# Three token tiles under the first expert's weights, and a PSUM bank shared with the adapter, in a two-layer conditional kernel

## The reference

```python
# layer 0: 8 gated experts and one shared expert, all applied to all tokens, F = 512
g = einsum('bsd,edf->ebsf', h, Wg);  u = einsum('bsd,edf->ebsf', h, Wu)
expert_outs = einsum('ebsf,efd->ebsd', silu(g) * u, Wd)
expert_output = einsum('be,ebsd->bsd', gating_probs, expert_outs)
shared = einsum('bsf,fd->bsd', silu(h @ Sg) * (h @ Su), Sd)
x = x + (1 - sg) * expert_output + sg * shared
# layer 1: an adapter per sequence, its weights chosen by language_ids; then a layer norm with gamma, beta
h1 = relu(x @ W1[lang] + b1[lang])
z = x + h1 @ W2[lang] + b2[lang]
x = x + layernorm(z) * gamma[lang] + beta[lang]
```

## Time and profile before

| | |
|---|---|
| median of 3 runs | 305.44 us (305.38 to 305.45) |
| the profiled execution, its own time | 304.87 us |
| its span, first to last instruction | 303.1 us |
| TensorE matmul busy | 295.1 us, 97% of the span |
| VectorE busy | 264.4 us, 87% |
| ScalarE busy | 226.6 us, 75% |
| GpSimd busy | 15.9 us, 5% |
| mean granted TensorE clock | 0.996 of full speed |

### The profile page before, as it was taken

One profiled execution on the slowest core, in us unless ns is written; L12 is line 12 of the kernel. 1 busy time (PEld: TensorE's weight loads), 2 busy tenths in 40 slices (PEclk: granted clock), 3 DMA queues, 4 the chain that ended last, 5 costly groups with the idle time before them and its releaser, 6 DMA issues.

```text
span 303.1 us, 4961 instructions
## 1 busy us (share of the span) xinstructions
PE 295.1 (97%) x1532; PEld 147.5 (49%) x1532; DVE 264.4 (87%) x590; ACT 226.6 (75%) x505; POOL 15.9 (5%) x24
## 2 busy tenths in 40 slices
PE   8999999999999999999999999999999999999983
PEld 3344444444444444444444444444444444688862
DVE  5999999998989898987779998699987899888894
ACT  5897878788878787877677776777777676688761
POOL 0200101200000000000010100101001010000000
PEclk9999999999999999999999999999999999999998
DMA  7990000014400000000000010000000000100000
GB/s 248 414 404 11 0 0 2 9 38 121 121 11 0 2 0 0 0 2 2 0 8 13 0 37 0 1 14 7 35 0 2 10 9 0 37 1 2 3 17 17
DMA packets 9133, 12.12 MB, mean 40 GB/s; under 512 B 3843, under 2 KB 6804, under 8 KB 9108
## 3 DMA queue, kind: packets, MB, share of 16 engines
q1 hardware_dynamic: 8962, 11.75, 11.3%
q10 hardware_dynamic: 146, 0.07, 0.1%
HBM read 10.76 MB, written 1.05 MB: 39 GB/s over the span
## 4 chain that ended last, share of the span: by engine, by line
PE 89%; issue 3%; DVE 1%; POOLq 0%; POOL 0%; DVEq 0%; ACT 0%
PE moe_ps L328 10%; PE moe_ps L330 10%; PE gate_ps L287 10%; PE moe_ps L327 10%; PE up_ps L309 10%; PE up_ps L312 10%; PE gate_ps L293 10%; PE gate_ps L290 10%; PE up_ps L306 10%; PE adapt_ps L353 1%; PE adapt_ps L340 1%; PE x_ps L345 1%; DVE hidden L500 0%; DVE h_lo L506 0%; DVE gx_lo L481 0%
## 5 line engine op out<-in xcount | busy, mean ns | idle before, releaser
L426 ACT ACTIVATE silu<-gate_ps 128x512 f32<-128x512 f32 (+1 forms) x160 | 88.6, 554 | 64.1 <-PE gate_ps L293 63.5
L500 DVE SCALAR_TENSOR_TENSOR hidden<-silu,up_ps 128x512 f32<-128x512 f32 (+1 forms) x160 | 100.7, 630 | 28.7 <-PE up_ps L312 22.6
L506 DVE TENSOR_TENSOR h_lo<-hidden,h_hi 128x512 f16<-128x512 f32 (+1 forms) x160 | 101.5, 635 | 0.1
L431 ACT ACTIVATE h_hi<-hidden 128x512 f16<-128x512 f32 (+1 forms) x160 | 92.8, 580 | 2.5 <-DVE hidden L500 2.2
L330 PE MATMUL moe_ps<-h_lo,w_hi 128*128 128x512 f16 (+1 forms) x160 | 57.3, 358 | 0.9 <-DVE h_lo L506 0.8
L309 PE MATMUL up_ps<-gx_lo,w_hi 128*128 128x512 f16 (+1 forms) x160 | 57.3, 358 | 0.7 <-DVE gx_lo L481 0.7
L287 PE MATMUL gate_ps<-x_hi,w_hi 128*128 128x512 f16 (+1 forms) x160 | 57.7, 360 | 0.0
L293 PE MATMUL gate_ps<-x_hi,w_lo 128*128 128x512 f16 (+1 forms) x160 | 57.5, 360 | 0.0
L290 PE MATMUL gate_ps<-x_lo,w_hi 128*128 128x512 f16 (+1 forms) x160 | 57.5, 360 | 0.0
L306 PE MATMUL up_ps<-gx_hi,w_hi 128*128 128x512 f16 (+1 forms) x160 | 57.3, 358 | 0.1
L327 PE MATMUL moe_ps<-h_hi,w_hi 128*128 128x512 f16 (+1 forms) x160 | 57.3, 358 | 0.0
(11 more groups left out here) (74 smaller groups left out, 146.4 us busy)
## 6 DMA issues: line engine op xcount, KB each, us to landing
w_full<-weights SPq DMA_DIRECT2D x8, 768.0 KB, 10.8
affine_sb<-affine SPq DMA_DIRECT2D x16, 128.0 KB, 2.9
x_full<-xT SPq DMA_DIRECT2D x4, 256.0 KB, 6.4
w_full<-weights SPq DMA_DIRECT2D x3, 256.0 KB, 4.3
out_dram<-result SPq DMA_DIRECT2D x3, 256.0 KB, 2.0
w2b_sb<-w2b SPq DMA_DIRECT2D x16, 16.5 KB
w_sb<-w SPq DMA_DIRECT2D x16, 16.0 KB
b_sb<-b SPq DMA_DIRECT2D x16, 0.1 KB
```

The costliest lines, as they stand in the source:

```text
L426: nc.scalar.activation(pair_slot(silu, n), gate_ps[n % 2][:, 0:STEPS[n][4]], ACT.Silu, scale=1.0 / W_SCALE).then_inc(silu_ready, 1)
L431: nc.scalar.activation(h_slot(h_hi, n), pair_slot(hidden, n), ACT.Copy).then_inc(h_hi_ready, 1)
L500: nc.vector.scalar_tensor_tensor(out=pair_slot(hidden, n), in0=pair_slot(silu, n), scalar=HIDDEN_RESCALE, in1=up_ps[n % 2][:, 0:STEPS[n][4 ...
L506: nc.vector.tensor_tensor(h_slot(h_lo, n), pair_slot(hidden, n), h_slot(h_hi, n), ALU.subtract).then_inc(h_lo_ready, 1)
```

## The change

Expert 0 is applied to tiles 0, 1 and 2 before expert 1 is begun; tile 2 so has its first group as steps 8 to 11, and all groups of tiles 0 and 1 with experts 1 to 8 come one group later. The count of groups, steps and matmuls stays. The weights of expert 1 are converted at steps 6, 8 and 10, not at 4, 5 and 6; those of the later experts keep their place within the turn. Tile 2 must be loaded and split early, so its load moves ahead of the load of expert 1, and `X_AFTER[2]` falls from 9 to 3. Tile 2's sum begins while those of tiles 0 and 1 are still open, so it gets a bank of its own, `moe_ps2`, and the adapter writes into `moe_ps0`, which is free from the end of tile 0 on. The second half of tile 3 uses tile 2's bank. Because `JOBS` is worked out from the steps, the jobs of tiles 0 and 1 start 4 steps later.

```diff
-GROUPS = [(t, e) for e in range(NE) for t in (0, 1)] + [(2, e) for e in range(NE)] + [(3, e) for e in range(NE)]
+FIRST = [(t, 0) for t in (0, 1, 2)]
+GROUPS = (FIRST + [(t, e) for e in range(1, NE) for t in (0, 1)] + [(2, e) for e in range(1, NE)]
+          + [(3, e) for e in range(NE)])
...
-W_AT = {2 * CHUNKS * e + s: (e + 1, third) for e in range(NE - 1)
-        for third, s in enumerate((4, 5, 6) if e == 0 else (2, 4, 6))}
-
-X_AFTER = {1: 2, 2: 9, 3: 12}
+W_AT = {s: (1, third) for third, s in enumerate((6, 8, 10))}
+W_AT |= {CHUNKS * (len(FIRST) + 2 * (e - 1)) + s: (e + 1, third) for e in range(1, NE - 1)
+         for third, s in enumerate((2, 4, 6))}
+
+X_AFTER = {1: 2, 2: 3, 3: 12}
...
-        moe_ps = [bank("moe_ps0"), bank("moe_ps1")]
-        adapt_ps = bank("adapt_ps")
+        moe_ps = [bank("moe_ps0"), bank("moe_ps1"), bank("moe_ps2")]
+        adapt_ps = moe_ps[0]
...
-        last_moe_ps = moe_ps[0]
+        last_moe_ps = moe_ps[2]
...
-            return moe_ps[0] if at > 0 else moe_ps[t % 2]
+            return last_moe_ps if at > 0 else moe_ps[1 if t == TILES - 1 else t]
...
             sp.dma_start(cols(w_full, 2, F), weights[0, :, 2 * F:]).then_inc(w0_loaded[2], 16)
+            sp.dma_start(cols(x_full, 2, N), xT[2]).then_inc(x_loaded[2], 16)
             for e in range(1, NE):
                 sp.dma_start(cols(w_full, e, W_COLS), weights[e]).then_inc(w_loaded[e - 1], 16)
-                if e in (2, 3):
-                    sp.dma_start(cols(x_full, e, N), xT[e]).then_inc(x_loaded[e], 16)
+                if e == 3:
+                    sp.dma_start(cols(x_full, 3, N), xT[3]).then_inc(x_loaded[3], 16)
...
-                if f == 0 and e == 0 and t > 1:
-                    pe.wait_ge(x2T_ready, t - 1)
+                if f == 0 and e == 0 and t == TILES - 1:
+                    pe.wait_ge(x2T_ready, 2)
...
-                nc.vector.scalar_tensor_tensor(out=x2T[:, :], in0=moe_ps[t % 2][:, :], scalar=OUT_RESCALE,
+                nc.vector.scalar_tensor_tensor(out=x2T[:, :], in0=moe_bank(t, 0)[:, :], scalar=OUT_RESCALE,
```

## The result

The changed kernel takes 306.11 us (median of 7 runs, 305.86 to 306.45) against 305.38 us (7 runs, 304.87 to 305.45); the ratio worked out from all runs of both is 1.0029, 95% interval 1.0019 to 1.0039 (the quotient of the two medians alone is 1.0024). Of the twelve runs of experiment 3, two took 522.31 and 1771.03 us, for a reason that no trace here shows; its ratio leaves them out. The profiled execution has a span of 304.1 us, 303.1 before.

What follows compares the result with a forecast made beforehand. TensorE was taken to bound the kernel, with VectorE's lateness before 13.81 us having no slack. The collision's +1.00 us and zero for all else, added to 305.44, gave 306.44 us, range 305.4 to 306.9.

Steps and rivals of the forecast that it cites:

- What bounds the kernel: TensorE 97% busy, gapless from 14.70 to 285.00 us; at step 4 it loses about 0.7 us waiting for VectorE.
- the last critical quarters: Group 1's last gx_lo quarters on VectorE, ending at 13.81 us; step 4's second up matmul waits for them.
- The collision: GpSimd's early split of tile 2, from 10.49 us, holds VectorE's h_lo 0.10 and gx_lo 0.90: +1.00 us.
- The rival of the full lock: Both GpSimd instructions hold VectorE for their whole length near 10.5 us: +1.38, total 306.82 us; chance 0.14.
- Edits costed at nothing: Order, matmul count, loads, banks, jobs and later conversions of expert 1's weights: each claimed to cost or gain 0.
- the relief at steps 4 and 5: Converting expert 1 later lightens VectorE and ScalarE where TensorE never waits: gain 0; rival that it counts, 304.75 us, chance 0.04.
- the nearest of the covers: Tile 2's adapter weights, issued until 213.4 us and wanted at 228.69 + 1.0: covered by 16 us, cost 0.
- The sum: Total +1.00 us on the median of 305.44 us: 306.44 us, 0.33% slower.
- the likeliest case: Whole kernel at 306.44 us, with its own range from 306.1 to 306.8; chance 0.57.
- the tail's clock is safe: Between 294 and 297 us TensorE is busy 1.62 of 3.00 us, clock 1.00; rival of falling clock, 309.2 us, chance 0.04.

Runs made afterwards that it cites:

- experiment 3: Changed kernel with only GpSimd's subtraction for tile 2 held back until group 1's gx_lo is done, its copy left early; 305.46 us, ratio 1.0001.
- experiment 1: Changed kernel with GpSimd's whole split of tile 2 held back until group 1's last gx_lo quarters are done; 305.44 us, ratio 1.0000.
- experiment 2: Kernel before with two edits alone: tile 2's x loaded right behind expert 0, and X_AFTER[2] = 3; 306.52 us, ratio 1.0034.
- experiment 7: Kernel before with X_AFTER[2] = 3 alone, tile 2's x still loaded behind expert 2; 305.95 us, ratio 1.0037.
- experiment 6: Changed kernel with expert 1's weights converted at steps 4, 5 and 6 as before, not at 6, 8 and 10; 306.43 us, ratio 1.0038.

## Why the prediction was right

- *What bounds the kernel.* TensorE without a gap from step 4 on, VectorE without slack before it: experiments 1, 2 and 7 put nearly the same loss of VectorE (1.02, 0.99 and 0.90 us) after, before and just at the last critical quarters, and the total followed the place alone.
- *The collision.* Predicted copy at 10.49, `hidden(2)` at 13.01, pair at 14.21, second up matmul at 14.86; measured 10.49, 12.99, 14.19, 14.85. The loss of 1.00 us, taken from the earlier trace rows, was 0.98. The trace of before held the same four instructions in the same phase; where the phase was another, in experiment 7, the loss was 0.90. The rival of the full lock, +1.38, is refuted: the lock is there, but it lets the leads of experiment 3 through.
- *Edits costed at nothing.* Order, banks, jobs, loads, and the relief at steps 4 and 5: experiments 1 and 6 confirm zero. Tile 2's adapter weights, the nearest of the covers, were issued until 213.70 and wanted at 229.67:

```profile
213.70 0.32 SPq L262 DMA_DIRECT2D b_sb<-b  x1
```

- *The sum.* 306.44 was forecast, 306.11 measured. Most runs of a sample lie near one of two levels: those of before near 304.88 and 305.45, those of after near 305.86 and 306.45, with 305.21, 306.11 and 306.29 in between. Level against level the change costs 0.98 and 1.00 us; the medians of 7 give 0.73. The forecast added 1.00 to a median of three runs that all lay on the upper level, and this choice was not argued. That the measured median still lies within the likeliest case's own range, at its lower edge of 306.1, depends on how the seven runs fell and not on the mechanism.
- *What I had wrong.* That the tail's clock is safe: I argued from the earlier trace rows that the granted clock stays at 1.00 although TensorE is busy only 1.62 of 3.00 us there. Experiment 1's tail shows it falling after just such a stretch. It didn't touch this prediction, because the idle stretches that the change makes, 0.57 and 0.66 us at step 4, left the clock at 1.00. TensorE's busy time from 8.6 to 15.7 was forecast at 5.5 us and came to 5.87. The forecast had added the whole 1.00 to the idle time; but a matmul that stands alone between two waits counts as busy for its 0.38 us and not for the 0.22 to the next start. The rest is that TensorE's short wait at step 3 had gone and its stream reached step 4 0.11 us later (below).

## What to carry to other kernels

A wait count that releases a GpSimd instruction is also a choice of which VectorE instructions it will hold; look at what VectorE does just then and how much slack it has. Held here were those with all inputs in SBUF; `hidden`, with one in PSUM, kept its 0.68 us beside both GpSimd instructions. The cost of a moved collision could be read here off the place in the trace where the same instructions already collide, to a few hundredths, because the phase agreed. And where TensorE waits for one of two results that VectorE makes one after the other, try their order first: one swap was worth 0.5 us of the span here, about 0.2%, the whole regrouping nothing.

## What the runs showed of the hardware that was not expected

**The clock can fall in the tail.** In the last steps TensorE works with gaps. In the profile of before the granted clock was still 1.00 between 297 and 298 us, in that of experiment 1, with the same tail, it was 0.65 (the column before the last two):

```profile
297.00:298.00 1.00, 1.00 (x9) 0.66 (x8) 0.31 (x2) 0.68 (x2) 0.00 (x0) 1.00 0.00 0
```

```profile
297.00:298.00 1.00, 1.00 (x7) 0.83 (x7) 0.17 (x1) 0.69 (x2) 0.00 (x0) 0.65 0.00 0
```

After it the clock was 0.50, that is 1.2 GHz, and the span 0.8 us longer; experiment 6's profile shows the same fall. The idle times of TensorE before it were no longer than 0.48 us each. That the two levels of the timed runs, some 0.57 us apart, are this fall, is not shown, because those runs have no trace, and it can't be all of it. Each run has its mean granted clock on record. Of the 25 runs of the kernel before that stand beside experiment 1, the ten at 304.87 to 304.90 us had 0.996 to 0.998. Eleven of the fifteen slower ones had 0.989 to 0.994, which fits a fall in the tail (0.989 in experiment 1's profile), but four, at 305.21 to 305.45, had 0.998 or 0.999. And in the sample of the changed kernel the four slower runs had the higher clock, 0.997 or 0.998 against 0.995 or 0.996. A late rise at the start, which follows, could be behind these; no trace shows one that costs so much.

**A late rise of the clock costs nothing at first.** Matmuls 0.43 us apart went on until about 6.8 us in the profile of before and until 8.5 in experiment 3. In the changed kernel `hidden(0)` started at 8.82, 0.39 later than before, and yet `hidden(1)` at 10.28 as before: the conversion between them, 0.93 us long instead of 1.32, waited for GpSimd's subtraction of tile 1 (until 9.81) in both. The collision at 9 us hid the late clock, and TensorE's short wait at step 3 went with it. This cover has an end. In the seven profiles where the slow matmuls ended by 8.0, `hidden(1)` starts at 10.27 or 10.28; where they went on to 8.4 or 8.5 (experiments 6 and 3) at 10.36 and 10.37, and in experiment 7, where they went on to 8.6, here:

```profile
10.47 0.68 DVE L500 SCALAR_TENSOR_TENSOR hidden<-silu,up_ps 128x512 f32<-128x512 f32 x1
```

From there on each tenth is lost, because nothing covers VectorE's work until the last quarters of `gx_lo`.
